# Attention and a quantised feed-forward layer on one core: score tiles of a group placed side by side in TensorE's order, and two PSUM banks for the last batch's output products

## The reference

```
x  = x + attention(xn) + ffn(xn)
attention: qkv = xn @ w_qkv; windows of 4 rows, one every 2 rows; 8 heads of 64;
           softmax(q k^T * 512**-0.5) v in each window; @ w_out + b_out;
           the windows' rows are added back where they came from
ffn:       gate, up = q4(xn) @ q4(w_gate)^T, q4(xn) @ q4(w_up)^T   (512 -> 1408)
           out = q4(silu(gate) * up) @ q4(w_down)^T                 (1408 -> 512)
q4: each block of 16 is rounded to FP4 (E2M1) values with a scale of its own
```

## Time and profile before

| | |
|---|---|
| median of 3 runs | 2204.44 us (2202.26 to 2205.87) |
| the profiled execution | 2204.8 us, of which the span from first to last instruction is 2202.7 us |
| TensorE busy | 2148.9 us (98%) |
| VectorE busy | 1663.7 us (76%) |
| GpSimd busy | 1219.0 us (55%) |
| ScalarE busy | 656.9 us (30%) |
| TensorE clock granted | 1.000 of full speed |
| attention, with the head | to 829 us |
| feed-forward layer | from 829 us on |
| one pass of the loop | 98.4 to 99.4 us |

### The profile page before, as it was taken

The page is one execution under the profiler, slowest core; times in us unless marked ns, Lnnn a source line. Parts: engine busy times, 40 slices in busy tenths (PEclk is TensorE's granted clock), DMA queues, the critical chain, the costliest instruction groups (busy, mean ns, idle before and its releaser), DMA issues.

```text
span 2202.7 us, 46918 instructions
## 1 busy us (share of the span) xinstructions
PE 2148.9 (98%) x16712; PEld 1037.8 (47%) x16712; DVE 1663.7 (76%) x3108; ACT 656.9 (30%) x1009; POOL 1219.0 (55%) x877
## 2 busy tenths in 40 slices
PE   4999999999999989999999999999999999999999
PEld 1544444544444444444444444444444444444444
DVE  7877877787787666877878778787787777878774
ACT  2342433333343322222222222222222232222221
POOL 3256767666665554555555555555555555555553
PEclk9999999999999999999999999999999999999999
DMA  9656656575766544333333333433334333343333
GB/s 267 189 122 175 157 142 175 133 191 133 177 149 167 136 166 111 82 87 83 78 90 80 87 83 78 94 75 87 86 80 91 77 83 89 77 92 74 87 74 68
DMA packets 449418, 251.82 MB, mean 114 GB/s; under 512 B 367282, under 2 KB 373938, under 8 KB 449300
## 3 DMA queue, kind: packets, MB, share of 16 engines
q1 hardware_dynamic: 448404, 246.99, 46.1%
q10 hardware_dynamic: 576, 2.10, 0.2%
q0 software_dynamic: 320, 0.97, 0.2%
HBM read 99.01 MB, written 59.77 MB: 72 GB/s over the span
## 4 chain that ended last, share of the span: by engine, by line
PE 75%; POOL 10%; issue 9%; DVE 2%; DMA 1%; SPq 0%; ACT 0%; POOLq 0%; DVEq 0%; ACTq 0%
PE acc L978 10%; PE prj L1350 7%; PE ops L1350 7%; PE acc L1331 5%; PE acc L1335 5%; PE acc L1332 5%; PE prj L978 3%; PE ops L1352 3%; PE prj L1352 3%; PE sps L1333 2%; PE acc L1334 2%; PE sps L1336 2%; PE acc L1336 2%; PE sps L1334 2%; PE acc L1333 2%
## 5 line engine op out<-in xcount | busy, mean ns | idle before, releaser
L978 PE MATMUL acc<-late 128*128 128x512 f16 x2304 | 516.8, 380 | 11.0 <-DMA late<-xh 10.9
L978 PEld LDWEIGHTS acc<-late 128*128 128x128 f16 x2304 | 218.4, 98 | 270.7 <-issue 16.5
L209 POOL TENSOR_TENSOR qk<-qk,xh 128x1408 f32<-128x1408 f32 x64 | 165.6, 2588 | 230.1 <-DVE qk L246 230.1
L1225 DVE SCALAR_TENSOR_TENSOR qk<-acc,row_gains,xh 128x512 f32<-128x512 f32 x64 | 48.0, 751 | 260.2 <-ACT xh L1290 260.2
L204 POOL TENSOR_TENSOR qk<-qk,xh 128x1024 f32<-128x1024 f32 (+1 forms) x128 | 177.3, 1386 | 111.2 <-DVE xh L225 111.2
L214 POOL TENSOR_TENSOR v<-qk,v 128x1408 f16<-128x1408 f32 x64 | 183.0, 2859 | 100.3 <-ACT v L256 100.3
L1350 PE MATMUL prj<-late,qk 128*128 128x512 f16 x704 | 214.6, 379 | 0.7 <-DMA qk<-v 0.7
L1350 PE MATMUL ops<-late,qk 128*128 128x512 f16 x704 | 214.6, 379 | 0.0
L256 ACT ACTIVATE v<-qk 128x1408 f16<-128x1408 f32 x64 | 88.1, 1377 | 367.3 <-POOL qk L209 367.3
L1331 PE MATMUL acc<-late,turned 128*128 128x512 f16 x512 | 194.0, 379 | 0.4 <-DVE qk L1225 0.4
L1335 PE MATMUL acc<-late,turned 128*128 128x512 f16 x512 | 194.1, 379 | 0.0
(11 more groups left out here) (158 smaller groups left out, 4440.0 us busy)
## 6 DMA issues: line engine op xcount, KB each, us to landing
normed<-late SPq DMA_DIRECT2D x64, 256.0 KB, 3.0
res<-in_L_attn_x SPq DMA_DIRECT2D x64, 256.0 KB, 2.9
attended<-res SPq DMA_DIRECT2D x64, 256.0 KB, 2.5
raw<-normed SPq DMA_DIRECT2D x64, 256.0 KB, 2.7
v<-attended SPq DMA_DIRECT2D x64, 256.0 KB, 2.7
out<-v SPq DMA_DIRECT2D x64, 256.0 KB, 2.0
late<-in_L_attn_x SPq DMA_DIRECT2D x62, 256.0 KB, 3.8
ready<-turned SPq DMA_DIRECT2D x36, 256.0 KB
```

Source lines behind the costliest of these rows:

```text
L209: pool.tensor_tensor(blocks(v), blocks(v), spread(s[3]), ALU.mult).then_inc(q["valued"], 1)
L978: last = pe.matmul(out, lhsT, rhs, start=(at == 0), stop=(at == n - 1))
```

## The change

In the loop's string on TensorE, score tiles of a group are moved side by side: s0, s1 and s2 stand directly ahead of a6 (s0 stood ahead of a5 and s1 ahead of p1), s3 moves from behind q14 to behind a8, s5 from ahead of v4 to ahead of s4, and s6 and s7 stand beside s8. v1 is now ahead of a5, and p1 directly behind a5. Head and tail strings and the strings of all other engines stay as they are. In the last batch the output products with an odd number go to `acc[2]` and the even ones stay in `prj`; a product there waits for `final` of two tiles back, not of one, and p1 waits for all copies out of the `acc` banks. The feed-forward layer's second product group, which reuses `acc[2]`, waits also for the last `final`.

```
@@ attention
+    def out_bank(b, i):
+
+
+        return acc[2] if isinstance(b, int) and b == B - 1 and i % 2 else prj
+
@@ finish
-            dve.scalar_tensor_tensor(res[:, i % 4, :], prj[:, :], sc[:, 5:6], res[:, i % 4, :],
+            dve.scalar_tensor_tensor(res[:, i % 4, :], out_bank(b, i)[:, :], sc[:, 5:6], res[:, i % 4, :],
@@ project_out
             pe.wait_ge(o_lo, at(b, TPB, i))
-            pe.wait_ge(final, at(b, TPB, i - 1))
-            three_products(prj[:, :], [((oh[:, i % 4, 0, k], oh[:, i % 4, 1, k]),
+            if isinstance(b, int) and b == B - 1:
+                pe.wait_ge(final, at(b, TPB, max(i - 2, -1)))
+                if i == 1:
+                    pe.wait_ge(qkv_out, at(b, QKV, QKV - 1))
+            else:
+                pe.wait_ge(final, at(b, TPB, i - 1))
+            three_products(out_bank(b, i)[:, :], [((oh[:, i % 4, 0, k], oh[:, i % 4, 1, k]),
                                                (wo[:, 0, k], wo[:, 1, k])) for k in range(KC)]).then_inc(proj_done, 1)
@@ batches(pe, ...)
-                "p6' s5 v4 s4 a0 v5 a1 s6 p7' s7 v6 s8 v7 a2 q0+ q1+ q2+ a3 q3+ q4+ q5+ a4 q6+ q7+",
-                "v0+ p0 s0+ a5 v1+ s1+ p1 s2+ a6 v2+ p2 a7 v3+ q8+ q9+ q10+ q11+ p3 q12+ q13+ p4 a8 q14+ s3+ p5 q15+",
+                "p6' v4 s5 s4 a0 v5 a1 p7' v6 s6 s7 s8 v7 a2 q0+ q1+ q2+ a3 q3+ q4+ q5+ a4 q6+ q7+",
+                "v0+ p0 v1+ a5 p1 s0+ s1+ s2+ a6 v2+ p2 a7 v3+ q8+ q9+ q10+ q11+ p3 q12+ q13+ p4 a8 s3+ q14+ p5 q15+",
@@ feed_forward
-    acc_free = [ended.copied, ended.copied + ended.masked, ended.masked + ended.evacuated]
+    acc_free = [ended.copied, ended.copied + ended.masked + ended.projected, ended.masked + ended.evacuated]
```

## The result

The change made the kernel slower: 2212.83 us median of 7 runs (2210.26 to 2215.49) against 2205.59 us (2201.5 to 2209.4) for the kernel before, a ratio of 1.0033 with a 95% interval of 1.002 to 1.0045. I had predicted 2205.3 us and a range to 2209.5. The profiled run has a span of 2210.8 us against 2202.7, so +8.1 us.

The account below looks back on a forecast made before the run. TensorE, busy 98% of the span, was taken as the bound, with little to win from waits. Loop +3.2 us (+5.0 and -1.8) and last batch -2.3 us sum to +0.9, so 2205.3 us, range 2200 to 2209.5.

Parts of the forecast that it names:

- What limits p1: Loop: p1 waits for f0, late from DVE's backlog, and starts 0.15 us after it, so it can hardly come earlier.
- f0's offsets: Loop passes 1 to 6: f0 ends 6.30, 7.55, 8.84, 6.55, 8.18, 7.08 us after p0's start.
- signs of being wrong: f0 over 0.7 us earlier relative to p0, the row of 192 over 2.5 us, or a changed feed-forward length.
- The end of s2 is what counts next: Loop: m0 on DVE starts on s2's end, then f1, then p2; s2 ends later, together +5.0 us.
- f0's offset + 0.15 + 2.70 + 3 x 0.69: Loop: end of s2 after p0's start, with p1 at 2.70 us and three score tiles at 0.69 us each.
- Merging saves entries: Loop: 10 bursts instead of 14, 0.1 us per entry; three entries outside p0 to p2 save 1.8 us.
- Rival 3: Loop: merging saves no entry, the 0.1 us is paid at each tile; 2207.7 us, chance 0.10.
- Rival 1: Five score-tile joints a pass: each tile costs 0.93 instead of 0.69 us, 7.2 us in all; 2212.5 us, chance 0.13.
- The last batch: Tail: a6 stays at 807.53, waits before p3 to p6 go, p7 starts at 824.3 instead of 826.60: -2.3 us.
- The feed-forward layer: After the attention: its 1370 us are not touched, and the last batch's gain passes through to the end.

Follow-up runs that it names:

- the run with the banks alone: Kernel before with only the two banks for the last batch's output products, all strings as before: 2202.76 us, ratio 0.9996.
- The experiment with the other groups alone: Kernel before with only s3 moved behind a8, s5 beside s4, s6 and s7 beside s8: 2204.58 us, ratio 0.9999.
- the fillers: Changed kernel with unused matmuls of 128x128 ahead of p1 in the loop: 20 in fp16, 2253.1 us; 4 in fp32, 2223.47 us.
- the shift: 17 fp32 matmuls (68 instructions) at the program's start: changed kernel 2234.27 us; kernel before 2203.9 us; changed kernel with p1 behind s0 s1 s2, 2212.33 us.
- f0 early in it: Changed kernel with f0 moved ahead of R1 and d2 on DVE in the loop: 2206.18 us, ratio 1.0011.
- the small filler: Changed kernel with 4 unused fp32 matmuls of 128x128 (16 instructions) ahead of p1 in the loop: 2223.47 us, ratio 1.0082.
- first group alone: Kernel before with only v1 ahead of a5, p1 directly behind a5, and s0 s1 s2 side by side ahead of a6: 2213.08 us, ratio 1.0036.
- p1 last: Changed kernel with p1 moved behind s0 s1 s2 and ahead of a6 in the loop: 2213.51 us, ratio 1.0035.
- the last version: Kernel before with s0 s1 s2 merged ahead of p1, 17 fp32 matmuls at the start, and the two banks: 2201.74 us, ratio 0.9987.

## Why the prediction was wrong

- **What limits p1: right.** f0 sets p1's start, not TensorE's stream. The sum of f0's offsets came out as said (44.5 us), but that is luck: single passes are off by -1.1 to +0.8 us, and the run with the banks alone, whose loop is that of the kernel before, has offsets of 5.2 to 9.0 us with a sum of 43.8 where that kernel had 45.9. So f0 did come over 0.7 us earlier in two passes, one of my signs of being wrong. p1 followed f0 by 0.15 us in passes 2 to 6; in pass 1 f0 was 1.1 us earlier than I had it, and p1 started at 5.90 us, the limit of the stream.
- **"The end of s2 is what counts next": right in direction, the price was wrong.** I had +5.0 us for p0 to p2, and it was +12.1. Of the 7.1 us between, p1's clock is 4.9 (rows of 4.44, 4.26 and 4.44 us instead of 2.75), p1's start 0.5, the way from a6 to p2 1.15, which I had kept unchanged, and the break in a score run 0.5. **The step that failed is the one that priced p1's wait as idle time alone:** in "f0's offset + 0.15 + 2.70 + 3 x 0.69" the term 2.70, p1 itself, measured about 4.3 us (1.5 to 1.7 more) in passes 2, 3 and 5. I had written down waits of 0.5 to 2.4 us at p1, and they came; I did not ask what a gap of over 2 us does to the clock behind it. No row of the kernel before has such a gap followed by a product: its longest wait at an output product is 1.42 us. That the gap and the low clock belong together is borne out by all 14 profiles: from the loop's first pass to the end of the attention 36 products ran slow, and each has an idle time of 0.93 us or more in it or at most two steps ahead of it.
- **Merging saves entries (-1.8 us outside this stretch): wrong.** The stretches outside p0 to p2 sum to 503.8 us before and 504.0 after. The timeline of TensorE has these rows for s6 s7 s8 in pass 6, and the product behind them:

```profile
703.61 2.59 PE L1030 MATMUL sps<-qk 64*32 64x32 f32 x192
706.13 2.76 PE L983 MATMUL acc<-late 128*128 128x512 f16 x12
```

  s6 s7 s8 take 2.52 us from start to start here and 2.4 to 2.9 us over the six passes, and not 2.1; my row of over 2.5 us as a sign of being wrong is there. s4 starts 0.71 us after s5 in four passes and 0.85 to 0.87 in two, but a0 starts 0.8 to 1.4 us after s4, where it was 0.8 to 0.9. The first merged run takes 2.05 (2.1 to 2.2 us to the start of a6 in the five passes without a break), so 0.69 us a tile is right there. The experiment with the other groups alone, ratio 0.9999, says the same. Rival 3 had the size right, not the reason: the first run pays nothing at its joints.
- **Rival 1, score tiles starving one another** gave 2212.5 us, 0.3 us from the result, but not for its reason: it wanted 0.24 us at every joint, 7.2 us in all. All joints together cost about 2 us (+0.2 where I had -1.8). Its idea, that a long run of small instructions outruns what feeds TensorE, is what the fillers and the shift showed, with another pattern: nothing at the joints of the first run, and 0.7 to 2.5 us at one fixed place.
- **The last batch: somewhat better than said.** -3.6 us against -2.3. a6 came 6.27 us after p0, where it was 7.38 (to 807.53); I had kept it. This too is luck: it hangs on the second half of d3, DVE's step on L779 between f0 and f1, which h3, o5 and so a6 wait for. It stands there beside a POOL step or slips in ahead of it. Where it takes 0.18 us (the changed kernel, f0 early in it, the small filler), a6 comes 6.27 us after p0; where it takes 1.29 us (the six other profiles with two banks), 7.1 to 7.4 us. p7 waits 1.36 us for POOL, as the prediction has it (timeline of the changed kernel, p4, p5 and p7):

```profile
826.95 2.75 PE L983 MATMUL acc<-wo,oh 128*128 128x512 f16 x12
829.54 2.75 PE L983 MATMUL prj<-wo,oh 128*128 128x512 f16 x12
...
833.65 2.76 PE L983 MATMUL acc<-wo,oh 128*128 128x512 f16 x12 [1.36 <-POOL oh L579]
```

- **The feed-forward layer: nearly untouched.** It is 1.0 us longer; its first product group waits 1.4 us for DVE in all, where it was 0.4. The prediction had the gain of the last batch pass through to the end; the banks themselves take this 1.0 us back, as the run with them alone shows. A changed length of this layer was one of my signs of being wrong.

The sum of the four differences (loop +9.1, head -1.7, tail -1.3, feed-forward layer +1.0) is +7.1 us, which is the way from +0.9 predicted to +8.0 in the profiles (8.1 from the rounded spans).

**What stays open.** Idle times of 2.45 us (first group alone, pass 4) and 2.47 us (p1 last, pass 6) were followed by products at full clock, and ones of 1.51 us (the last version, pass 3), 1.06 us (the shift, s8 at 514.60 us) and 0.93 us (the small filler, v7 in pass 2) were not: length alone doesn't decide, and I can't say what does. The supply of instructions is inferred from places and sums; nothing in the trace shows it at work, and I did not count the register instructions of a pass. It also doesn't explain the whole: s6 s7 s8 and s4 with a0 are up to 0.8 us longer without a break in them, in small gaps spread over the run. And with the shift the place also falls into a0 with 15 matmuls left, 290 small instructions behind the last product, yet in twelve passes (the shift on the changed kernel and on the one with p1 last) there is one break of 0.54 us; breaks in every pass were seen from 312 small instructions on. How the loss divides between the waits and the clock is known from one profile only (4.9 us of 8.1 for the clock); the run with f0 early loses both at once, and neither filler had an f0 as late as the changed kernel's, so no run separates them.

## What to carry over

Before you let a busy TensorE wait in one piece where it used to wait in several, price the product behind the gap at half clock as well, and keep in mind that a wait which stays the same in sum may move to where it does that. Don't string together tiles of many small matmuls: a product between them cost nothing here, and by the runs above it gives the instructions time to arrive; if you must, try the kernel with a few instructions added at its start, since what you measure may be the place and not the idea. And before you call a filler a test of an idle time, look whether the idle time would still be there: here f0 came in time by itself, it seems because the kernel had become slower elsewhere.

## What the runs showed of the hardware

- A gap of 0.9 to 2.5 us on TensorE was often, not always, followed by the low clock: 0.50 of full speed, 1.2 GHz, and 12 matmuls in 3.83 to 4.45 us instead of 2.75, 1.1 to 1.7 us lost beside the gap. With gaps of 1.55 and 1.69 us in the changed kernel it stayed at 1.00. No product behind the head of the attention ran slow without such a gap, in 14 profiles.
- Runs of small matmuls (192 with their weight loads in 2.05 us) can outrun their own instructions, as far as places and sums tell. The break comes at the same matmul in each pass, at places about 256 instructions apart; it costs 0.7 to 2.5 us where 312 or more small instructions stand in a row ahead of it (and at most five matmuls of the next product after them), and 0 to 0.8 us where a product of 2.65 us lies 290 or fewer back, or nine matmuls of the next one are through. From the 1.4 us that 256 small instructions take, and breaks of 1.57 to 2.47 us behind them, I estimate 3 to 4 us from one piece to the next.
- 17 matmuls ahead of everything moved the total of the changed kernel by 21 us (2212.8 to 2234.3), and that of the kernel before by nothing (ratio 0.9999).
- A small step on DVE (128x32 in fp32, L779 or L774) took 0.18 us where no POOL step was running around it, and 1.19 to 1.30 us in the cases above, ending within 0.06 us of a POOL step's end (so did all 401 steps of this kind that last over 1 us, in 14 profiles). It moved a6 of the last batch by 1.1 us and p2 of the loop by about 1 us.
